# A two-layer-normed transformer block with self- and cross-attention: P*V sums added on the way out of PSUM, the output projection in 64-row tiles behind tile 6, and VectorE's order around the bursts

## The reference

```python
def _attention(xq, xkv, wq, wk, wv, wo, bo):
    q = (xq @ wq).reshape(B, S, N_HEADS, D_HEAD)
    k = (xkv @ wk).reshape(B, T, N_HEADS, D_HEAD)
    v = (xkv @ wv).reshape(B, T, N_HEADS, D_HEAD)
    attn = jax.nn.softmax(jnp.einsum("bihd,bjhd->bhij", q, k) * scale, axis=-1)
    out = jnp.einsum("bhij,bjhd->bihd", attn, v).reshape(B, S, D_ATTN)
    return out @ wo + bo
h = _layernorm(x, ln1_g, ln1_b)
x = _attention(h, h, sa_wq, sa_wk, sa_wv, sa_wo, sa_bo) + x
h = _layernorm(x, ln2_g, ln2_b)
x = _attention(h, cond_emb, ca_wq, ca_wk, ca_wv, ca_wo, ca_bo) + x
h = _layernorm(x, ln3_g, ln3_b)
p = h @ ff_w1 + ff_b1
a, gate = (p[..., :D_FF], p[..., D_FF:])
return (a * jax.nn.gelu(gate, approximate=False)) @ ff_w2 + ff_b2 + x
```

## Time and profile before

| | us |
|---|---|
| median of three executions | 1070.79 |
| profiled execution, its own time | 1067.25 |
| its span | 1065.5 |
| TensorE busy (L602 297.2, L627 239.7, L639 134.4) | 1025.8 |
| VectorE busy (L1174 314.9, L1169 307.9) | 831.1 |
| ScalarE busy (L947 285.8, L966 106.5) | 626.1 |
| mean granted clock of TensorE, share of full | 0.997 |

### The profile page before, as it was taken

The page is one execution under the profiler, slowest core; times in us unless marked ns, Lnnn a source line. Parts: engine busy times, 40 slices in busy tenths (PEclk is TensorE's granted clock), DMA queues, the critical chain, the costliest instruction groups (busy, mean ns, idle before and its releaser), DMA issues.

```text
span 1065.5 us, 28582 instructions
## 1 busy us (share of the span) xinstructions
PE 1025.8 (96%) x12258; PEld 834.5 (78%) x12258; DVE 831.1 (78%) x971; ACT 626.1 (59%) x1127; POOL 307.7 (29%) x280
## 2 busy tenths in 40 slices
PE   7999999999998999999999999998998998999998
PEld 5777777777776788777777777776687988888887
DVE  4778888889889888888888889898868898645433
ACT  4756666666666666666665666675755644443322
POOL 5102322323232123423223223221314357701000
PEclk9999999999999999999999999999999999999999
DMA  9896676577666866675785667597210001100000
GB/s 187 235 207 158 136 154 150 126 141 148 130 138 123 193 128 132 125 167 118 145 181 116 128 136 153 116 224 150 46 61 21 1 21 50 31 1 20 20 2 39
DMA packets 178366, 121.37 MB, mean 114 GB/s; under 512 B 142656, under 2 KB 158528, under 8 KB 173760
## 3 DMA queue, kind: packets, MB, share of 16 engines
q1 hardware_dynamic: 177280, 116.40, 50.7%
q0 software_dynamic: 960, 3.15, 1.0%
HBM read 56.60 MB, written 12.58 MB: 65 GB/s over the span
## 4 chain that ended last, share of the span: by engine, by line
PE 80%; DVE 7%; ACT 5%; issue 4%; POOL 2%; DMA 1%; SPq 0%; DVEq 0%; ACTq 0%; POOLq 0%
PE W L627 21%; PE SC L602 18%; PE W L639 10%; PE SC L691 8%; PE W L575 7%; PE W L701 4%; PE W L585 4%; PE W L867 3%; ACT OTF L955 3%; PE SC L679 2%; DVE nmax L1169 2%; DVE PR L1174 2%; POOL PR L515 1%; PE W L854 1%; ACT PR L947 1%
## 5 line engine op out<-in xcount | busy, mean ns | idle before, releaser
L947 ACT ACTIVATE PR<-SC,nmax 128x1024 f32<-128x1024 f32 x256 | 285.8, 1116 | 224.6 <-DVE nmax L1169 224.1
L1169 DVE TENSOR_REDUCE nmax<-SC 128x1 f32<-128x1024 f32 x256 | 307.9, 1203 | 107.8 <-PE SC L602 107.6
L1174 DVE STREAM_TRANSPOSE PR<-PR 128x1024 f32<-128x1024 f32 x256 | 314.9, 1230 | 0.1
L464 POOL TENSOR_TENSOR X<-f_raw,X 128x512 f32<-128x512 f32 x128 | 165.0, 1290 | 497.1 <-ACT f_raw L966 497.0
L602 PE MATMUL SC<-QKS 128*128 128x512 f32 x1024 | 297.2, 416 | 5.3 <-ACT PR L947 4.8
L627 PE MATMUL W<-PR,V 32*64 32x256 f32 x8192 | 239.7, 379 | 3.5 <-DMA V<-scratch_v 2.3
L602 PEld LDWEIGHTS SC<-QKS 128*128 128x128 f32 x1024 | 184.2, 188 | 65.3 <-issue 23.5
L627 PEld LDWEIGHTS W<-PR,V 32*64 32x64 f32 x8192 | 187.1, 132 | 49.9 <-issue 22.6
L639 PE MATMUL W<-wo,OTF 128*128 128x256 f32 x512 | 134.4, 385 | 8.2 <-ACT OTF L955 7.2
L639 PEld LDWEIGHTS W<-wo,OTF 128*128 128x128 f32 x512 | 93.9, 189 | 37.3 <-ACT OTF L955 21.1
L966 ACT ACTIVATE f_raw<-W,rden 128x256 f32<-128x256 f32 x256 | 106.5, 473 | 0.1
(11 more groups left out here) (130 smaller groups left out, 1410.9 us busy)
## 6 DMA issues: line engine op xcount, KB each, us to landing
QKS<-QKT SPq DMA_DIRECT2D x64, 512.0 KB, 6.3
V<-scratch_v SPq DMA_DIRECT2D x128, 256.0 KB, 5.0
QKS<-QKT SPq DMA_DIRECT2D x128, 128.0 KB, 4.9
scratch_v<-VST SPq DMA_DIRECT2D x32, 256.0 KB, 4.7
wo<-in_L_xattn_sa_wo_dram SPq DMA_DIRECT2D x64, 64.0 KB, 3.0
f_raw<-in_L_xattn_ff_w_dram POOLq DMA_DIRECT2D x12, 256.0 KB, 3.3
X<-in_x_dram SPq DMA_DIRECT2D x4, 512.0 KB, 4.9
w_raw<-in_L_xattn_sa_wk_dram SPq DMA_DIRECT2D x16, 128.0 KB, 3.0
```

The lines of the kernel that those rows point to most:

```text
L464: nc.gpsimd.tensor_tensor(xs, f_raw[:, k % 2, :], xs, ALU.add).then_inc(p_x, 1)
L947: nc.scalar.activation(PR[:, NT * s + t, :], SC[t % 2][:, :], ACT.Exp, bias=nmax[:, t % 4:t % 4 + 1], accum_out=den[:, s, t:t + 1]).then_i ...
L1169: V.tensor_reduce(nmax[:, t % 4:t % 4 + 1], SC[t % 2][:, :], AX, ALU.max, negate=True).then_inc(d_max, 1)
L1174: V.transpose(tile, tile).then_inc(d_tr, 1)
```

## The change

1. **P*V sums** (`attend`, both `gather`s). Odd key blocks now write W's columns 128 to 383 of a bank instead of 0 to 255. ScalarE makes two copies of 64x512: the even sums' first half goes to OTH's partitions 64 to 127, the odd sums' last half to partitions 0 to 63. VectorE then adds W's middle columns and OTH into OTF, now 128x512, in which partitions 64 to 127 hold rows of tiles 0 to 3 and partitions 0 to 63 those of tiles 4 to 7, already summed over even and odd. TensorE waits for this add (`d_ot`).
2. **Output projection** (`project_out`). Two steps of two column groups, each of two matmuls that contract over 64 partitions, one in the upper and one in the lower half of the array, into different banks. In most heads both steps stand behind the scores of tile 6. In seven heads (`IN_TWO`) the second stands at tile 0 of the next head. V projections and transpositions at tile 5 wait for `d_ot`.
3. **ScalarE** scales steps 0 and 1 ahead of exp 6 and the other two ahead of exp 0 (exp 1 for `IN_TWO`) of the next head.
4. **VectorE** transposes tile 2 ahead of row maximum 3, tiles 3 and 4 behind row maximum 4, then does the add.
5. **SyncE** stores the second k/v weights behind the first V loads instead of ahead of them.
6. Banks of the last head and of the following stage are changed to suit (`MB`, `out_bank`).

```diff
-        STEPS = {5: 0, 6: 1, 7: 2}
-        OUT_BANK = (2, 1, 0, 1)
+        OUT_TILE = (4, 0, 6, 2)
+        IN_TWO = (0, 11, 12, 13, 14, 29, 30)
+        def out_bank(h, n):
+            return ((1, 0, 0, 1) if h in IN_TWO else (2, 1, 0, 3) if h == HS - 1 else (3, 2, 1, 0))[n]
...
-            sp.wait_ge(a_pre, 8)
-            sp.dma_start(KV_d[1], flat(14, 2)).then_inc(m_kvs, 16)
             stored(0)
             load_v(0)
             load_v(1)
+            sp.wait_ge(a_pre, 8)
+            sp.dma_start(KV_d[1], flat(14, 2)).then_inc(m_kvs, 16)
...
+                    place = slice(P * (blk % 2), P * (blk % 2) + 2 * P)
                     for a in range(4):
                         rows = slice(Q * a, Q * a + Q)
-                        last = mm(W[cols, a, 0:2 * P], V4[s][rows, blk, :],
+                        last = mm(W[cols, a, place], V4[s][rows, blk, :],
...
-            def project_out(h, k):
-                if k == 0:
-                    pe.wait_ge(a_ot, h + 1)
+            def project_out(h, step):
+                if step == 0:
+                    pe.wait_ge(d_ot, h + 1)
                     pe.wait_ge(m_wo[h % 2], 32 * (h // 2 + 1))
                 for i in range(2):
-                    t = 2 * k + i
-                    last = mm(W[:, OUT_BANK[k], D * i:D * i + D], OTF[:, t * P:(t + 1) * P], wo2[h % 2][:, :],
-                              start=True, stop=True)
-                last.then_inc(s_op, 1)
+                    cols = slice((2 * step + i) * P, (2 * step + i + 1) * P)
+                    for c in range(2):
+                        rows = slice(DH * c, DH * c + DH)
+                        last = mm(W[:, out_bank(h, 2 * step + c), D * i:D * i + D], OTF[rows, cols],
+                                  wo2[h % 2][rows, :], start=True, stop=True)
+                        if i == 1:
+                            last.then_inc(s_op, 1)
...
-                    if h > 0 and t in STEPS:
-                        project_out(h - 1, STEPS[t])
+                    if h > 0 and t == 6:
+                        project_out(h - 1, 0)
+                        if h - 1 not in IN_TWO:
+                            project_out(h - 1, 1)
...
             def gather(h):
                 act.wait_ge(s_pv, 8 * (h + 1))
                 if h > 0:
-                    act.wait_ge(s_op, 4 * h)
-                nc.scalar.copy(OTF[:, :].rearrange("p (t a i) -> p a t i", a=4, i=Q),
-                               W[:, :, 0:2 * P].rearrange("p a (t i) -> p a t i", i=Q)).then_inc(a_ot, 1)
+                    act.wait_ge(d_ot, h)
+                for to, of, col in ((DH, 0, 0), (0, DH, 2 * P)):
+                    nc.scalar.copy(OTH[to:to + DH, :].rearrange("p (a n) -> p a n", a=4),
+                                   W[of:of + DH, :, col:col + P]).then_inc(a_ot, 1)
...
+            def gather(h):
+                dve.wait_ge(a_ot, 2 * (h + 1))
+                if h > 0:
+                    dve.wait_ge(s_op, 4 * h)
+                V.tensor_tensor(OTF[:, :].rearrange("p (t a i) -> p a t i", a=4, i=Q),
+                                W[:, :, P:2 * P].rearrange("p a (t i) -> p a t i", i=Q),
+                                OTH[:, :].rearrange("p (a t i) -> p a t i", a=4, i=Q), ALU.add).then_inc(d_ot, 1)
...
+                    if h > 0 and t == 3:
+                        turn(h, 2)
                     rowmax(h, t)
```

More of the change, by code:

```diff
@@ L748, in _ @@
                             pe.wait_ge(d_hl, 8)
-                        elif t == 0:
-                            pe.wait_ge(a_op, 4 * (h - 2) + 1)
+                        elif t == 0 and h - 2 not in IN_TWO:
+                            pe.wait_ge(a_op, 4 * (h - 2) + 2)
+                        elif t == 7 and h > 1 and h - 1 not in IN_TWO:
+                            pe.wait_ge(a_op, 4 * (h - 1) + 1)
                         elif h == 0 and t < 7:
@@ L756, in _ @@
                             pe.wait_ge(d_hl, 4 + 2 * (h - NH + 4) + 1)
-                        elif h > 0 and (h, 5) in V_AT:
+                        elif t == 7 and h > 0 and (h, 5) in V_AT:
                             u, i, _ = V_AT[h, 5]
@@ L780, in _ @@
                         turn_wq(i, bank)
-                    if t == 0 and h > 1:
+                    if t == 0 and h - 2 in IN_TWO:
                         pe.wait_ge(a_op, 4 * (h - 2) + 2)
-                        project_out(h - 2, 3)
+                        project_out(h - 2, 1)
             pe.wait_ge(a_op, 4 * (HS - 2) + 2)
-            project_out(HS - 2, 3)
+            project_out(HS - 2, 1)
             pe.wait_ge(m_kb[0], 16)
@@ L798, in _ @@
             ca_scores(1)
-            for k in range(4):
-                if k == 3:
-                    pe.wait_ge(a_op, 4 * (HS - 1) + 2)
-                project_out(HS - 1, k)
+            for step in range(2):
+                project_out(HS - 1, step)
             pe.wait_ge(m_vb[0], 16)
@@ L1029, in _ @@
                         gather(h - 1)
-                    if t in (6, 7) and h > 0:
-                        scale_out(h - 1, t - 6)
-                    if t in (0, 1) and h > 1:
-                        scale_out(h - 2, 2 + t)
+                    if t == 6 and h > 0:
+                        scale_out(h - 1, 0)
+                        scale_out(h - 1, 1)
+                    if h > 1 and t == (1 if h - 2 in IN_TWO else 0):
+                        scale_out(h - 2, 2)
+                        scale_out(h - 2, 3)
                     for g, n, bank in proj_before(h, t):
@@ L1259, in _ @@
                         split_qkv(g, n, W[:, bank, :])
-                    if t > 0 or h > 0:
+                    if h == 0:
+                        if t > 0:
+                            turn(h, t - 1)
+                    elif t not in (3, 5):
                         turn(*divmod(NT * h + t - 1, NT))
+                    if h > 0 and t == LAST_BURST:
+                        turn(h, t)
+                        gather(h - 1)
                     if h > 0 and t == 1:
```

33 lines of the change are left out of this document (18 added, 15 removed).

## The result

The changed kernel takes 1076.4 us (median of 9 runs, 1069.7 to 1082.9); the kernel before, run beside it, 1069.2 (1065.9 to 1073.3). The ratio is 1.0062, 95% interval 1.0035 to 1.0089: slower by 4 to 10 us, where 1048 and "faster" were forecast. The profiled execution took 1072.61 us around a span of 1070.7; before it was 1067.25 around 1065.5.

The account below looks back on a forecast made before the run. TensorE, busy 96%, bounds the kernel at 23.20 us a head; after the change two loops of 22.07 bind. Terms -22.0 + 0 + 0.9 + 2.8 - 0.6 - 4.0 = -22.9 take 1070.79 to 1048 us, range 1036 to 1068.

Parts of the forecast that it names:

- twenty heads with V at tile 1: Normal heads with their V projection at tile 1: 22.1 us each instead of 23.20, 1.1 gained a head, -22.0.
- three without V (11, 27, 28): Heads without a V projection: 22.01 before, 22.07 after by the loop through ScalarE that holds no V, counted as 0.
- V at tile 5 (1, 14, 15): Heads whose V projection waits for the add: second burst to next first burst 18.95 becomes 19.2, +0.3 each, +0.9.
- transpositions (12, 13, 30, 31): Heads with transpositions at tiles 5 and 6, two more evictions each on ScalarE inside the loops: 0.7 each, +2.8.
- last head and tail: Last head's projection stands alone; at most 1.7 of its 3.44 goes, the scalings behind hold most of it: -0.6.
- start: Head 0's V loads go 2.1 to 2.6 earlier, first burst shortens by 1.7 without a clock drop: -4.0 together.
- Rival (b): Output projection: pairs don't run side by side, 3.44 in one lump, 23.3 a head, 1081 us, slower; 14%.
- rival (c): VectorE's add costs 1.2, or the loops take 0.6 more elsewhere: 22.7 a head, 1066 us; 14%.
- The loops: Two once-a-head cycles of waits through TensorE, ScalarE and VectorE, each 22.07, longer than TensorE's own 21.7.
- Other heads: Step pricing heads unlike the twenty normal ones: 0 without V, +0.9 V at tile 5, +2.8 transpositions, -0.6 last head.
- Loop 1: Cycle from S0 (tile 0's scores) to next S0, through bursts, copies, add, row maximum 5, exp 5, scalings, exp 6: 22.07.

Follow-up runs that it names:

- experiment 12: Changed kernel with both matmuls of each projection pair on the same half of the array: 1102.45 us in one execution, a normal head 23.71.
- experiment 5: Changed kernel, from head 2 on each scaling does only its first of two activations: head with V at tile 1 takes 22.04, against 22.41.
- experiment 6: Changed kernel, from head 2 on VectorE's addition covers 128 of the 512 columns: head with V at tile 1 takes 22.04, against 22.41.
- experiment 7: Changed kernel, from head 2 on with half of each scaling and three quarters of the addition left out: head 21.66; 1045.6 us in one execution.
- experiment 1: Kernel before, with only the second k/v store moved behind the first V loads: 1069.04 us, ratio 0.9991 to the kernel before.
- experiment 10: As experiment 9, but the second k/v store again ahead of head 0's V loads: 1062.59 us, ratio 0.9934 to the kernel before.
- experiment 2: Changed kernel; in heads 1, 12 to 15, 30, 31 ScalarE's tile-6 scalings stand behind the copies TensorE waits for: 1067.05 us, ratio 0.997 to the kernel before.
- experiment 3: Changed kernel; in heads 1, 12 to 15, 30, 31 TensorE's tile-5 work stands behind the scores of tile 6: 1068.47 us, ratio 0.998 to the kernel before.
- experiment 8: Mixed: changed kernel, but head outputs 0, 8, 10 to 14 and 25 to 30 go the old way: 1053.99 us, ratio 0.9841 to the kernel before.
- experiment 9: As experiment 8, but output 31 the old way with the old tail, outputs 8 and 25 the changed way: 1057.51 us, ratio 0.9897 to the kernel before.
- experiment 11: Changed way only for outputs 0, 10 to 14, 26 to 31, old way elsewhere, store moved: 1086.43 us, ratio 1.0165 to the kernel before.

## Why the prediction was wrong

It was wrong in direction: slower by 7.2 us by the medians, where 22.9 faster was forecast with 83% for "faster". The terms against the two profiles, whose spans are 5.3 apart, in us:

| term | forecast | trace |
|---|---|---|
| twenty heads with V at tile 1 | -22.0 | -12.6 |
| three without V (11, 27, 28) | 0 | +2.2 |
| V at tile 5 (1, 14, 15), without the first burst's length | +0.9 | +6.8 |
| transpositions (12, 13, 30, 31) | +2.8 | +9.1 |
| head 29 | not in the sum | +2.5 |
| last head and tail | -0.6 | +1.1 |
| start (2.07 earlier, burst 1.69 shorter) | -4.0 | -3.8 |
| sum | -22.9 | +5.3 |

**What held.** The pairs overlap: 2.00 for both steps, and 3.72 without the pairing. Rival (b) is refuted; its price, 23.3 a head, was near the 23.7 of experiment 12. The addition lasts 0.69 with 0.61 to the next: rival (c) is refuted. The loops bind before TensorE does, by the three kernels of experiments 5 to 7. The start's rows came as forecast up to the end of the first burst; the stall behind it (0.94, 1.18 in experiment 1) stands in the table among the heads with V at tile 5, in head 1. That a wait at the start brings a lowered clock isn't a rule either: experiment 10 has the wait of 2.32 and no drop.

**The step that failed: "Other heads".** I priced the V-at-5 heads along one path, from V at +5.80 by four scalings, V's copy and exp 6 to S0 at +12.6, and from there with the durations of before, 19.2 in all; and the transposition heads by adding 0 to 0.98 to that. The trace has 20.82. The path forgot TensorE's own order: the k projection stands ahead of S0, and it waits for V's copy (1.04), or for the split behind the transposition's two operations (2.16 in heads 12 and 13). Before, that copy stood behind one scaling lump of 0.71 and TensorE didn't wait; now it stands behind four activations, 1.44, which themselves wait for a projection that has moved behind tile 6. So S0 comes at +13.3. From there to the next first burst it takes 7.5 instead of 6.6: outputs written in two rounds have their last scalings behind exp 0, for which the next V waits (0.32), and a V whose weights weren't loaded ahead takes longer. I had ScalarE's queue in the sum, but followed it to S0 alone and did not ask who else waits for what stands in it. Experiments 2 and 3 took away one wait each and got 9 to 10 us each, give or take 4; experiments 8, 9 and 11 show that the loss is local: +17.3 with the changed way in these heads alone, -16.0 and -11.6 where they go the old way.

Heads 11, 27 and 28, priced at 0, lost 2.2. Head 29 the prediction left out of its count; it waits 1.01, 0.92 and 2.31 for exps and stalls for 1.69, where before it waited 0.18 and 1.60 and stalled for 1.18.

**The granted clock.** I took a drop only for the start. Waits of 2.2 to 2.3 are followed by stretches at 0.50 in heads 12, 29 and 30, but the one of 2.16 in head 13 is not. What a stretch costs can be read where the work is the same and the clock isn't. Head 13 takes 27.60 here and 28.62 in experiment 11, with the same waits and one stretch at 0.50 there; and the first burst of the kernel before took 5.40 against 3.71. So a stretch costs 1.0 to 1.7 us, and of the +20.5 in these eleven heads the three stretches are some 3 to 5 us, an estimate; the rest is waiting, but for head 29's longer stall.

**The mis-sized term: V at tile 1.** Right mechanism, 22.07 forecast, 22.41 measured. Loop 1 by its pieces: forecast and trace agree within 0.02 for the burst, the row maximum, and exps and scalings together; the copies took 1.22 instead of 1.14; and S0 to the next burst took 5.90 instead of 5.57, since four matmuls whose weights aren't loaded ahead take 1.20 against 0.92, 0.28 and not the 0.10 I took. The third loop, through exp 5 and S7, I did not see; it stood at 22.04. Heads 9 and 26, where VectorE has statistics to compute as well, gained nothing (+0.25 and +0.27). That VectorE's list sets them is argued, not shown: over ten heads it is busy for 205.99 of 225.34 us. The same loops hold in heads without V, 22.53 instead of 22.04: experiments 5 and 6 bring head 11 to 21.79 and 22.13.

**The range.** It took in rival (b) alone on the slow side, as if a slower result could only come from normal heads. Ten special heads at 0.5 to 3 us each, against bounds of 0 to +1.3, should have been a rival of their own: it is the one that came true.

**Open:** what lasts of the start's gain; the tail, though the changed kernel's has a stretch at 0.50 (892.0 to 895.2) that the kernel before's hasn't, which by the price above may be all of its +1.1; head 28's +1.17, whose row is a wait of 1.99 for an exp, not traced further; and why the mixed kernel of experiment 9 isn't the faster one.

## What to carry to other kernels

When work on one engine gets shorter by giving another engine one more step, price the kinds of iterations one by one, and in the irregular ones walk down the in-order list of every engine that frees a buffer: ask of each item behind the lumped or moved instructions who waits for it, and what stands behind the one that waits. A scheme that pays in the regular iterations can be kept to them; here that turned +7 us into -16. And a chain of three loops of nearly the same length gives nothing when one is shortened: look for the piece that all of them share, here the addition.

## What the runs showed of the hardware

TensorE stalled inside bursts, waiting for nothing that the profile shows, and all such stalls of over 0.5 us were at one of three places of the program. In the second burst of head 1, with 48 matmuls left, it stood still for 0.64 to 2.72 in twelve kernels; not in the two whose first burst had waited for its data (the kernel before and experiment 10). In the second burst of head 29, with 97 to 103 left, it stalled in nine kernels: 1.18 in the kernel before, 1.69 in the changed one, 1.89 in experiment 1 and 3.41 in experiment 9. In five kernels (experiments 5 and 7 to 10) it came with 7 or 8 matmuls left in the first burst of head 19, for 2.6 to 3.2, at times from 475 to 486: a place in the program, not a time. The kernels before and after have none there, nor has experiment 6, quicker as it was. A granted clock of 0.50 followed in four of the five (484 to 487 above), but not in experiment 9, whose stall of 3.15 was the longest of them:

```profile
484.00:487.00 3.00, 3.00 (x92) 2.30 (x98) 2.86 (x3) 1.84 (x3) 0.00 (x0) 1.00 0.09 30
```

That it is instruction loading is a guess, and the trace doesn't favour it: the queue named "instruction" moved 0.03 to 0.05 MB around the stall, where the kernel before has 0.03 in the same window and experiment 6, without a stall, 0.05. The Trainium skill (Runtime: NRT & Kernel Launch, Instruction fetch mechanics) says the cost of crossing a block of instructions is mostly hidden; here a pause of 3 us was not hidden, whatever it is.
